# First layer's score maxima: one transpose of 24 columns per head pair and three small DMAs, in place of eight transposes of three columns

## The chip, the cores and the metric

The program runs on one core of a Trainium2 chip. The metric is the device time of one execution in microseconds. Matmuls and transposes run on TensorE (PE, its weight loads are shown as PEld), elementwise work on VectorE (DVE), ScalarE (ACT) and GpSimd (POOL); SyncE (SP) issues the DMAs.

## The reference

The input x is 8 sequences of 512 rows by 256 columns. Two layers follow each other: x + attention(layernorm(x)), x + ffn(layernorm(x)), and the same again with another attention and another ffn. What matters here is the first attention. It has 16 heads, queries of 96 values, and three sets of keys per head:

```python
a1 = _attn(q, k1, v1, causal=True)     # 512 latent keys
a2 = _attn(q, ks, vs, causal=False)    # 64 selected rows
a3 = _attn(q, kw, vw, causal=True)     # 512 window keys
out = g[:, 0] * a1 + g[:, 1] * a2 + g[:, 2] * a3
```

Each `_attn` is softmax(q k / sqrt(96)) v in float32, and a softmax over up to 512 keys must have its row's maximum (or something near it) taken off before the exponential. So there are 3 attentions x 2 heads x 4 blocks of 128 query rows = 24 columns of maxima for every pair of heads.

## The kernel before, in words

A hardware loop runs over the 8 sequences. Within a sequence the first attention goes by 8 pairs of heads, p = 0 to 7. Its scores are computed transposed: keys on the partitions, queries in the columns. A maximum therefore can't be taken off as a scalar per partition. It goes in as extra rows of the matmul: `QW[p % 2][0]` holds the queries' 96 values in partitions 0 to 95 (`D0` = 96), and in partitions 96, 97 and 98 the negated maxima of attentions A1, A3 and A2, each for 2 heads x 512 queries. The keys have a one in the row of their own attention, so that the 99-row product (L811) adds the negated maximum.

For pair p these are the steps:

- `max` (12 times, L774): scores of the pair in the other layout, of which DVE takes the maxima into `NMX[:, p % 2, 0:24]` (L1085, L1088, L1095). Column c = (attention * 2 + head) * 4 + query block.
- `mt` (`transpose_maxima`, L784): PE turns `NMX`. For each head there are four transposes of three columns (c, c + 8, c + 16), each of which writes 3 partitions x 128 columns of a bank of PSUM: 8 transposes in 2 banks.
- `mt_out` (`maxima_out`, L1419 for layer 1, through `copy` at L1340 for layer 0): ACT copies each bank (3 partitions x 512) straight into partitions 96 to 98 of `QW`.
- `unit` (12 times, L811 to L813): the transposed scores. Unit 0 of a pair waits first for the maxima to be in place, since it is the first to read them.
- ACT takes the exponential (L1445), POOL masks (L1573), and PE multiplies with the values (`pv`, L850).

Beside it, PE computes the next pair's queries and keys (`piece`, L731 to L745; their transposes `piece_tr`, L756). All engines walk the same list `STEPS[0]`, made once from numbers in `AFTER`: every engine has its own instructions of each step, in this order, and waits on semaphores. Within the list, what stands from `mt` up to the next `unit 0` is:

```
pair 0:       mt, tail_pe 3 (nothing), piece 2, mt_out, piece 3, piece_tr 0, unit 0
pairs 1 to 6: mt, piece 2, mt_out, unit 11 of the pair before, piece 3, pv 4, piece_tr 0, out, out, unit 0
pair 7:       mt, mt_out, unit 11 of the pair before, pv 4, out, out, unit 0
```

The banks of PSUM for scores and transposes are a ring of 5 (`Banks`): each use waits until the use 5 before it has been read. SP's queue in a sequence holds, in this order: the weights of pairs 1 and 2 (two DMAs of 256 KB each, L576 and L577), the store of the sequence before (512 KB, L573, in step `tail 3`, just ahead of `mt_out` of pair 0), and then the weights of pair p + 2 after piece 6 of each pair. `tail_pe` is the last layer of the sequence before, which is finished within the first attention of the next one.

Of the kernel before, what the change touches and what calls it, by code (L numbers as in the profile page):

```python
# [11 lines left out]
F32 = mybir.dt.float32  # L12
BF16 = mybir.dt.bfloat16
F32R = mybir.dt.float32r
# [243 lines left out]
def plan_banks():  # L258
    work, first, last = Banks(NWORK), Banks(NWORK), Banks(NWORK)

    def piece(banks, s):
        banks.use(s, 2 if s[0] == "piece_tr" or PIECES[s[2]][0] == "nv" else 4)

    def tail(banks, tag, j):
        for name in (["o0", "o1"], ["hT0", "hT1"], ["sign0", "sign1"], [])[j]:
            banks.use((tag, name))

    def prologue(banks, tag, j):
        for name in (["hT0", "hT1"], ["small0", "small1", "imp"], ["score_cols", "gate"], ["nqT", "ckvT"],
                     ["pos"], ["selT"])[j]:  # L270
            banks.use((tag, name))

    def attention(layer):
        for s in STEPS[layer]:
            if s[0] == "mt" and layer == 0:
                for h in range(2):
                    work.use((0,) + s + (h,))
            elif s[0] in ("unit", "max", "mt", "out_tr", "group"):
                work.use((layer,) + s, {"unit": 0, "mt": 2}.get(s[0], 1))
            elif s[0] in ("piece", "piece_tr"):  # L280
                piece(work, s)
            elif s[0] == "projection":
                for i in range(2):
                    work.use(("proj", i))
            elif s[0] == "pro_pe":
                prologue(work, "next", s[1])
            elif s[0] == "tail_pe":
                tail(work, "before", s[1])

    for j in range(6):  # L290
        prologue(first, "first", j)
    for m in range(NPIECE):
        piece(first, ("piece", 0, m))
        piece(first, ("piece_tr", 0, m))
    for j in range(4):
        tail(last, "last", j)
    work.of.update(first.of)
    work.of.update(last.of)
    attention(0)
    for i in range(2):  # L300
        work.use(("hT", 1, i))
    for s in FFN_STEPS:
        if s[0] == "pro_pe":
            prologue(work, "next", s[1])
        elif s[0] != "pro":
            work.use(s)
    for what, n in QKV_STEPS:
        if what == "half":
            work.use(("hT", 2, n))
        elif what == "v":  # L310
            work.use(("v", n))
        elif what == "qk":
            work.use(("qk1", n), 2)
        else:
            for k in range(4):
                work.use(("heads", n, k), 2 if k < 2 else 1)
    attention(1)
    return work

# [31 lines left out]
def build_program(nc, x, w_small, w_imp, w_q, w_nv, w_kw, w_sel, w_proj, g_q, g_kv,  # L351
# [4 lines left out]
    with ctx:  # L356
        def sb(name, shape, dt=F32):
            return ctx.enter_context(nc.sbuf_tensor(name, shape, dt))
# [67 lines left out]
        STATE = NRM[:, :].rearrange("p (i n a) -> p i n a", i=2, n=4)  # L426
        R2 = PR
        NMX = sb("NMX", [P, 2, 24])
        NPART = sb("NPART", [P, 2])
        RSUM = sb("RSUM", [P, 3, NT, 4])  # L430

# [11 lines left out]
        def sem(name):  # L443
            return ctx.enter_context(nc.semaphore(name))
# [15 lines left out]
        kr_ready = sem("kr_ready")  # L460
        tok_ready = sem("tok_ready")
        max_ready = sem("max_ready")
        exp_ready = sem("exp_ready")
        exp_masked = sem("exp_masked")
        evacuated = sem("evacuated")
# [21 lines left out]
        def full(e, use, bank):  # L487

            ring, sems, banks = bank
            k, _, f, _, _ = ring.of[use]  # L490
            e.wait_ge(sems[k], f)
            return banks[k]

        WORK = (work, work_full, WB)

        def maxima_uses(layer, p):
            return [(0, "mt", p, 0), (0, "mt", p, 1)] if layer == 0 else [(1, "mt", p)]

        def end_pass(e, n):

# [7 lines left out]
        def was_read(e, ring, sems, use):  # L508

            k, _, _, r, _ = ring.of[use]  # L510
            e.wait_ge(sems[k], r)
# [46 lines left out]
        @block.sync  # L558
        def _(sp):
            sp.dma_start(X0[:, :, :], x_rows[:, 0:NT, :]).then_inc(x_loaded, 16)  # L560
            for dst, src in early_loads:
                sp.dma_start(dst, src).then_inc(early_loaded, 16)

            def next_pass():

                sp.wait_ge(finished, 4)
                sp.sem_clear(cleared)
                sp.sem_inc(next_sequence, 1)

            def store(tag, row_tile):  # L570
                for i in range(2):
                    was_read(sp, work, work_read, (tag, f"sign{i}"))
                sp.dma_start(out_rows[:, bass.ds(row_tile, NT), :], X2[:, :, :]).then_inc(x_stored, 16)  # L573

            def load_weights(p):
                sp.dma_start(WKW[:, p % 2, :, :], w_kw[p % NPAIR]).then_inc(kw_loaded[p % 2], 16)  # L576
                sp.dma_start(WSEL[:, p % 2, :, :], w_sel[p % NPAIR]).then_inc(sel_loaded[p % 2], 16)  # L577

            load_weights(0)
            for dst, src in late_loads:  # L580
                sp.dma_start(dst, src).then_inc(late_loaded, 16)
            next_pass()
            with sp.Fori(0, B) as seq:
                for p in (1, 2):
                    load_weights(p)
                for s in STEPS[0]:
                    if s[0] == "piece" and s[2] == NPIECE - 1 and s[1] + 2 <= NPAIR:

                        full(sp, s, WORK)
                        load_weights(s[1] + 2)  # L590
                    elif s == ("tail", 3):

                        store("before", ((seq + (B - 1)) % B) * NT)

                for i in range(2):
                    was_read(sp, work, work_read, ("proj", i))
                sp.dma_start(X0[:, :, :], x_rows[:, bass.ds(((seq + 1) % B) * NT, NT), :]).then_inc(x_loaded, 16)
                next_pass()
            store("last", (B - 1) * NT)
            sp.wait_ge(x_stored, 16 * (B + 1))  # L600
            sp.wait_ge(x_loaded, 16 * (B + 1))
# [3 lines left out]
        def _(pe):  # L605
            mm = nc.tensor.matmul

            def take(use, bank):

                ring, full_sems, banks, read_sems = bank  # L610
                k, free_at, _, _, exp_at = ring.of[use]
                if exp_at > 0:
                    pe.wait_ge(exp_ready, exp_at)
                elif free_at > 0:
                    pe.wait_ge(read_sems[k], free_at)
                return banks[k], full_sems[k]
# [160 lines left out]
            def transpose_maxima(layer, p):  # L777
                if layer == 0:
                    pe.wait_ge(max_ready, p + 1)
                    for h in range(2):  # L780
                        ps, done = take((0, "mt", p, h), W)
                        for t in range(NT):
                            c = h * NT + t
                            last = nc.tensor.transpose(ps[0:3, t * P:(t + 1) * P], NMX[:, p % 2, c:24:8], ID[:, :])  # L784
                        last.then_inc(done, 1)
                else:
                    was_read(pe, work, work_read, (1, "max", p, len(MAX_UNITS[1]) - 1))
                    ps, done = take((1, "mt", p), W)
                    for t in range(NT):
                        last = nc.tensor.transpose(ps[0:2, t * P:(t + 1) * P], NMX[:, p % 2, t:8:NT], ID[:, :])  # L790
                    last.then_inc(done, 1)

            def unit(layer, p, i):

                if i == 0:

                    for use in maxima_uses(layer, p):
                        was_read(pe, work, work_read, use)
                ps, done = take((layer, "unit", p, i), W)
                for n_part, (a, h, j, col) in enumerate(UNITS[layer][i]):  # L800
                    q0, keys = j * P, (KEEP if layer == 0 and a == A2 else P)
# [197 lines left out]
        def _(dve):  # L999
# [71 lines left out]
            def maxima(layer, p, i):  # L1071
                u = MAX_UNITS[layer][i]
                ps = full(dve, (layer, "max", p, i), WORK)
                if i == 0 and layer * NPAIR + p >= 2:

                    full(dve, maxima_uses(*((layer, p - 2) if p >= 2 else (0, NPAIR - 2 + p)))[-1], WORK)
                for n, (lo, hi, att, h, qt) in enumerate(u["segs"]):
                    if att is None:
                        dst = NPART[:, h:h + 1]
# [256 lines left out]
        def _(act):  # L1336
# [72 lines left out]
                read_work(copy(dst[0], src), ("piece_tr", p, m))  # L1409

            def maxima_out(layer, p):
                for h in range(2):
                    if layer == 0:
                        ps = full(act, (0, "mt", p, h), WORK)
                        read_work(copy(QW[p % 2][0][D0:D0 + 3, h, :], ps[0:3, :]), (0, "mt", p, h))
                    else:
                        ps = full(act, (1, "mt", p), WORK)

                        read_work(a.activation(QZ[2 * D1:2 * D1 + 2, p, h, :], ps[0:2, :], ACT.Copy,  # L1419
                                               scale=ID[0:2, h:h + 1]), (1, "mt", p))  # L1420

            def outputs(layer, n, att):

# [291 lines left out]
```

## Time and profile before

| | us |
|---|---|
| median of 3 runs | 3653.43 |
| lowest, highest | 3652.27, 3654.14 |
| the profiled execution's own time | 3649.1 |
| its span | 3647.2 |

The span is from the first to the last instruction in the trace. An instruction is given by its line in the kernel, what it writes and reads, and its duration. A weight load (PEld) runs beside the matmul ahead of it, and a matmul's shown duration overlaps with the next one's: the distance from start to start tells what one costs. The granted clock of TensorE is given as a share of full speed.

### The profile page before, as it was taken

To read this page: it belongs to the slowest core of one execution; us is meant where nothing else is said; L and a number is where in the kernel's file an instruction comes from. 1 tells how busy PE (TensorE), PEld (TensorE's weight loads), DVE (VectorE), ACT (ScalarE), POOL (GpSimd) and SP (SyncE) were. 2 spreads that over 40 slices of the span, in tenths; PEclk is the share of its full clock that TensorE was granted. 3 is DMA by queue.
4 is the path that set the end of the run, shared out by engine and by line. 5 is a ranking of instruction groups with operands and counts; after the bars stand their busy time and mean duration, and the time that the engine had idled before them with its cause. 6 is when DMAs were issued, how large, how long until landed. Compare 5 with 4: busy or idle time off the path is not lost.

```text
span 3647.2 us, 58951 instructions
## 1 busy us (share of the span) xinstructions
PE 3255.5 (89%) x20560; PEld 2312.3 (63%) x20560; DVE 2121.1 (58%) x7104; ACT 1576.1 (43%) x3457; POOL 942.5 (26%) x1840
## 2 busy tenths in 40 slices
PE   4999789997899978998789988899788997899978
PEld 3776557765677646776467765677556765577655
DVE  3565655547556475665756656565665556556565
ACT  1444345533454334552444525445253542544434
POOL 0222222223222222222222222122221223222232
PEclk8999889998999989999899999999999998999989
DMA  2000000000000000000000000000001000000000
GB/s 90 24 14 12 1 13 24 18 7 1 19 18 19 7 1 25 18 13 7 1 25 19 13 7 1 30 18 7 6 1 30 19 7 6 13 18 19 13 0 7
DMA packets 31438, 53.75 MB, mean 15 GB/s; under 512 B 3472, under 2 KB 13456, under 8 KB 30864
## 3 DMA queue, kind: packets, MB, share of 16 engines
q1 hardware_dynamic: 31120, 49.64, 4.3%
q8 instruction: 183, 3.00, 0.4%
q14 instruction: 135, 1.11, 0.1%
HBM read 44.91 MB, written 4.72 MB: 14 GB/s over the span
## 4 chain that ended last, share of the span: by engine, by line
PE 77%; DVE 14%; issue 4%; POOL 3%; ACT 2%; SPq 0%; DMA 0%; ACTq 0%; DVEq 0%; POOLq 0%
PE outs L850 14%; PE work L774 7%; PE work L735 6%; PE work L811 6%; PE work L756 6%; PE work L812 5%; PE work L813 5%; PE work L857 4%; DVE work L1085 3%; PE work L731 3%; PE work L740 2%; PE work L635 2%; PE work L815 2%; PE work L745 2%; PE work L784 2%
## 5 line engine op out<-in xcount | busy, mean ns | idle before, releaser
L1445 ACT ACTIVATE PR<-work 128x512 f32<-128x512 f32 (+1 forms) x1088 | 640.0, 597 | 577.8 <-PE work L813 478.0
L1085 DVE CUSTOM_DVE_ANT_0 work<-work,KEEPB 128x384 f32<-128x384 f32 (+3 forms) x1536 | 665.4, 479 | 76.1 <-PE work L774 75.0
L1573 POOL TENSOR_SCALAR_AFFINE_SELECT PR<-PR 128x256 f32<-128x256 f32 (+1 forms) x960 | 348.1, 366 | 958.0 <-ACT PR L1445 954.0
L774 PE MATMUL work<-BIG 96*128 96x448 f32 (+9 forms) x1664 | 432.3, 354 | 71.2 <-issue 32.7
L1069 DVE TENSOR_TENSOR BIG<-work,BIG 96x512 fp32r<-96x512 f32 (+1 forms) x455 | 285.4, 629 | 351.1 <-ACT BIG L1340 351.1
L1563 POOL TENSOR_TENSOR TOK<-AB 128x256 f32<-128x256 f32 (+1 forms) x325 | 218.9, 674 | 867.7 <-DVE AB L1039 845.0
L850 PE MATMUL outs<-PR,ONES 128*32 128x512 f32 (+4 forms) x2304 | 404.6, 458 | 0.0
L811 PE MATMUL work<-BIG 99*128 99x512 f32 (+4 forms) x1152 | 404.5, 351 | 0.0
L774 PEld LDWEIGHTS work<-BIG 96*128 96x128 f32 (+1 forms) x1664 | 269.8, 196 | 205.0 <-issue 121.8
L1038 DVE TENSOR_TENSOR AB<-work,COS 128x256 f32<-128x256 f32 (+2 forms) x357 | 150.0, 420 | 429.3 <-PE work L735 368.1
L812 PE MATMUL work<-BIG 96*128 96x512 f32 (+4 forms) x1152 | 382.2, 332 | 0.0
L813 PE MATMUL work<-BIG 96*128 96x512 f32 (+4 forms) x1152 | 381.8, 331 | 0.0
L1340 ACT ACTIVATE BIG<-work 96x512 fp32r<-96x512 f32 (+2 forms) x583 | 315.7, 551 | 78.2 <-PE work L756 74.8
L850 PE MATMUL outs<-PR,VV 128*32 128x512 f32 (+3 forms) x2048 | 337.8, 440 | 0.0
L1340 ACT ACTIVATE TOK<-work 128x128 f32<-128x128 f32 (+1 forms) x455 | 122.6, 270 | 454.0 <-DVE AB L1039 242.6
L756 PEld LDWEIGHTS work<-ID,TOK 128*96 128x96 f32 (+1 forms) x1690 | 174.2, 126 | 162.3 <-issue 74.4
L735 PE MATMUL work<-WKW,HT 128*128 128x256 f32 x1040 | 277.0, 389 | 0.0
L756 PE MATMUL work<-ID,TOK 128*96 128x128 f32 (+1 forms) x1690 | 262.7, 275 | 14.4 <-ACT VV L1340 8.1
L811 PEld LDWEIGHTS work<-BIG 99*128 99x128 f32 (+1 forms) x1152 | 210.4, 183 | 40.4 <-issue 24.3
L813 PEld LDWEIGHTS work<-BIG 96*128 96x128 f32 (+1 forms) x1152 | 213.1, 185 | 23.7
L1088 DVE TENSOR_REDUCE NMX<-work 128x1 f32<-128x64 f32 (+1 forms) x640 | 172.3, 285 | 85.1 <-PE work L774 79.8
L812 PEld LDWEIGHTS work<-BIG 96*128 96x128 f32 (+1 forms) x1152 | 212.9, 185 | 5.0
(166 smaller groups left out, 5457.9 us busy)
## 6 DMA issues: line engine op xcount, KB each, us to landing
WKW<-w_kw_dram SPq DMA_DIRECT2D x65, 256.0 KB, 2.7
WSEL<-w_sel_dram SPq DMA_DIRECT2D x65, 256.0 KB, 3.0
X<-x_dram SPq DMA_DIRECT2D x9, 512.0 KB, 3.4
out_dram<-X SPq DMA_DIRECT2D x9, 512.0 KB, 2.9
WFC<-w_fc_dram SPq DMA_DIRECT2D x1, 1024.0 KB, 10.3
WFP<-w_ffp_dram SPq DMA_DIRECT2D x1, 1024.0 KB, 12.1
WQKV<-w_qkv_dram SPq DMA_DIRECT2D x1, 768.0 KB, 13.2
WQ<-w_q_dram SPq DMA_DIRECT2D x1, 576.0 KB, 7.2
```

Source lines behind the costliest of these rows:

```text
L735: last = mm(ps[:, 192:448], HT0[:, c, t * P:(t + 1) * P], WKW[:, p % 2, c, :], start=(c == 0), stop=(c == NC - 1))
L756: last = nc.tensor.transpose(ps[0:D0, h * rows:(h + 1) * rows], TOK[0:rows, (nth(p) * NPIECE + m) % 4, h, :], ID[0:rows, 0:rows])
L774: last = mm(ps[:, col:col + n], q, k, start=(i_mm == 0), stop=(i_mm == len(u["mm"]) - 1))
L811: mm(out, k[0][0:D0 + 3], q[0][0:D0 + 3], start=(col == 0), stop=False)
L812: mm(out, k[0][0:D0], q[1][0:D0], start=False, stop=False)
L813: last = mm(out, k[1][0:D0], q[0][0:D0], start=False, stop=stop)
L850: last = mm(bank[row:row + 32, j * P:T], v, PR[0:rows, slot, col:col + T - j * P], start=(j == 0), stop=(j == 2 or a == A2), skip_group_ch ...
L1069: read_work(v.tensor_tensor(dst[1], src, dst[0].bitcast(F32), ALU.subtract), use)
L1085: last = v.tensor_tensor_reduce(ps[:, lo:hi], ps[:, lo:hi], KEEPB[:, T - (hi - lo):T], -1.0, -NEG, ALU.add, ALU.min, dst)
L1340: return a.activation(dst, src, ACT.Copy)
L1445: a.activation(PR[0:rows, j % NP, :], ps[0:rows, :], ACT.Exp).then_inc(exp_ready, 1)
L1573: gp.affine_select(blocks, blocks, [[0, len(cols)], [1, P]], ALU.is_ge, 0.0, base=0, channel_multiplier=-1).then_inc(exp_masked, 1)
```

## The change

One transpose turns all 24 columns of `NMX` into 24 partitions x 128 columns of one bank. ACT copies these into a new tile `MROWS` (24 partitions, 2 buffers). SP waits for the copy and issues three DMAs from SBUF to SBUF: attention a has partitions 8a to 8a + 7 of `MROWS` (2 heads x 4 blocks, 128 values each, 512 bytes), which become one row of 1024 values, 4 KB, in partition 96 + a of `QW`. Unit 0 waits on their semaphore. The place of `mt`, `mt_out` and `unit` in `STEPS` is as before; SP gets a branch for `mt_out`. Layer 1 computes as before.

```diff
             def transpose_maxima(layer, p):
                 if layer == 0:
                     pe.wait_ge(max_ready, p + 1)
-                    for h in range(2):
-                        ps, done = take((0, "mt", p, h), W)
-                        for t in range(NT):
-                            c = h * NT + t
-                            last = nc.tensor.transpose(ps[0:3, t * P:(t + 1) * P], NMX[:, p % 2, c:24:8], ID[:, :])
-                        last.then_inc(done, 1)
+                    ps, done = take((0, "mt", p), W)
+                    nc.tensor.transpose(ps[0:24, 0:P], NMX[:, p % 2, :], ID[:, :]).then_inc(done, 1)
...
             def maxima_out(layer, p):
+                ps = full(act, (layer, "mt", p), WORK)
+                if layer == 0:
+                    if p >= 2:
+                        act.wait_ge(maxima_placed, MAXIMA_PLACED * (p - 1))
+                    read_work(copy(MROWS[:, p % 2, :], ps[0:24, 0:P]), (0, "mt", p))
+                    return
                 for h in range(2):
-                    if layer == 0:
-                        ps = full(act, (0, "mt", p, h), WORK)
-                        read_work(copy(QW[p % 2][0][D0:D0 + 3, h, :], ps[0:3, :]), (0, "mt", p, h))
...
+            def place_maxima(p):
+                was_read(sp, work, work_read, (0, "mt", p))
+                for a in range(3):
+                    sp.dma_start(QW[p % 2][0][D0 + a:D0 + a + 1, 0:2, :].bitcast(F32),
+                                 MROWS[8 * a:8 * a + 8, p % 2, :].bitcast(F32)).then_inc(maxima_placed, 16)
...
+                    elif s[0] == "mt_out":
+                        place_maxima(s[1])
...
             def unit(layer, p, i):
                 if i == 0:
-                    for use in maxima_uses(layer, p):
-                        was_read(pe, work, work_read, use)
+                    if layer == 0:
+                        pe.wait_ge(maxima_placed, MAXIMA_PLACED * (p + 1))
+                    else:
+                        was_read(pe, work, work_read, (1, "mt", p))
...
-            if s[0] == "mt" and layer == 0:
-                for h in range(2):
-                    work.use((0,) + s + (h,))
-            elif s[0] in ("unit", "max", "mt", "out_tr", "group"):
-                work.use((layer,) + s, {"unit": 0, "mt": 2}.get(s[0], 1))
+            if s[0] in ("unit", "max", "mt", "out_tr", "group"):
+                work.use((layer,) + s, {"unit": 0, "mt": 1 + layer}.get(s[0], 1))
```

`MAXIMA_PLACED` is 16 * 3, the semaphore's count for three DMAs.

## Rows read from the trace of the kernel before

**Rows 1.** The page: busy time (us, share, instructions) and the chain's shares

```profile
PE 3255.5 (89%) x20560; PEld 2312.3 (63%) x20560; DVE 2121.1 (58%) x7104; ACT 1576.1 (43%) x3457; POOL 942.5 (26%) x1840
...
PE 77%; DVE 14%; issue 4%; POOL 3%; ACT 2%; SPq 0%; DMA 0%; ACTq 0%; DVEq 0%; POOLq 0%
```

**Rows 2.** Stretches: from:to length, busy by engine (instructions), clock, DMA share, GB/s

```profile
551.93:579.54 27.61, 27.56 (x188) 20.12 (x187) 16.62 (x60) 15.33 (x37) 7.21 (x16) 1.00 0.12 39
579.54:610.83 31.29, 31.29 (x228) 22.33 (x227) 19.10 (x69) 15.55 (x38) 8.90 (x19) 1.00 0.06 18
```

**Rows 3.** Groups by line: busy us, mean ns of one

```profile
L1340 ACT ACTIVATE TOK<-work 128x128 f32<-128x128 f32 x390 | 108.5, 278 | 367.6 <-DVE AB L1039 240.7 <-issue 89.5 <-PE work L740 19.5
...
L784 PE MATMUL work<-ID,NMX 128*3 128x128 f32 x512 | 66.4, 273 | 0.0
```

**Rows 4.** Timeline around pair 1's maxima: start, us, instruction, [idle before <-releaser]

```profile
579.33 0.96 PEld L784 LDWEIGHTS work<-ID,NMX 128*3 128x3 f32 x8
579.54 1.04 PE L784 MATMUL work<-ID,NMX 128*3 128x128 f32 x8
...
580.50 0.52 PEld L740 LDWEIGHTS work<-WQ,NQT 32*128 32x128 f32 x4 [0.22 <-issue]
...
581.25 0.28 ACT L1340 ACTIVATE TOK<-work 128x128 f32<-128x128 f32 x1 [0.28 <-PE work L740]
...
581.72 1.06 ACT L1340 ACTIVATE BIG<-work 3x512 fp32r<-3x512 f32 x2
...
584.56 0.19 PEld L811 LDWEIGHTS work<-BIG 99*128 99x128 f32 x1
```

**Rows 5.** Timeline around pair 0's maxima

```profile
551.93 1.04 PE L784 MATMUL work<-ID,NMX 128*3 128x128 f32 x8
...
554.11 1.06 ACT L1340 ACTIVATE BIG<-work 3x512 fp32r<-3x512 f32 x2
...
555.24 0.19 PEld L811 LDWEIGHTS work<-BIG 99*128 99x128 f32 x1
```

**Rows 6.** Timeline around pair 7's maxima

```profile
766.05 1.04 PE L784 MATMUL work<-ID,NMX 128*3 128x128 f32 x8
...
766.25 0.59 ACT L1445 ACTIVATE PR<-work 64x512 f32<-64x512 f32 x1 [1.26 <-PE work L813]
...
766.87 1.06 ACT L1340 ACTIVATE BIG<-work 3x512 fp32r<-3x512 f32 x2
...
768.71 0.19 PEld L811 LDWEIGHTS work<-BIG 99*128 99x128 f32 x1 [0.41 <-issue]
```

**Rows 7.** Timeline of SP's queue: start of the issue, us that it took

```profile
520.67 0.33 SPq L576 DMA_DIRECT2D WKW<-w_kw_dram  x1
521.04 0.43 SPq L577 DMA_DIRECT2D WSEL<-w_sel_dram  x1
521.51 1.31 SPq L576 DMA_DIRECT2D WKW<-w_kw_dram  x1
522.87 0.43 SPq L577 DMA_DIRECT2D WSEL<-w_sel_dram  x1
```

**Rows 8.** DMAs from 551.9 to 554.9: busy tenths in 40 slices, queue, landing

```profile
DMA  0000000000002899999999999999998300000000
...
q1 hardware_dynamic: 528, 0.52, 49.3%
...
out_dram<-X SPq DMA_DIRECT2D x1, 512.0 KB, 2.8
```

**Rows 9.** All loads of L576 (256 KB each)

```profile
DMA to landing us min/median/max: 2.4/2.7/5.6
```

**Rows 10.** Stretches in the second layer with PE partly idle, columns as in rows 2

```profile
877.00:882.80 5.80, 2.40 (x20) 1.93 (x19) 2.45 (x4) 5.36 (x11) 4.05 (x5) 1.00 0.00 0
882.80:886.20 3.40, 3.39 (x16) 2.99 (x15) 0.69 (x1) 3.03 (x6) 0.00 (x0) 0.50 0.00 0
886.20:899.90 13.70, 8.35 (x42) 5.64 (x44) 12.56 (x48) 5.38 (x11) 1.18 (x4) 1.00 0.01 2
```

More of the change, by code:

```diff
@@ L428, in build_program @@
         NMX = sb("NMX", [P, 2, 24])
+        MROWS = sb("MROWS", [24, 2, P], F32R)
         NPART = sb("NPART", [P, 2])
@@ L462, in build_program @@
         max_ready = sem("max_ready")
+        maxima_placed = sem("maxima_placed")
         exp_ready = sem("exp_ready")
@@ L494, in build_program @@
         WORK = (work, work_full, WB)
-        def maxima_uses(layer, p):
-            return [(0, "mt", p, 0), (0, "mt", p, 1)] if layer == 0 else [(1, "mt", p)]
+        MAXIMA_PLACED = 16 * 3
         def end_pass(e, n):
@@ L1074, in maxima @@
                 if i == 0 and layer * NPAIR + p >= 2:
-                    full(dve, maxima_uses(*((layer, p - 2) if p >= 2 else (0, NPAIR - 2 + p)))[-1], WORK)
+                    full(dve, (layer, "mt", p - 2) if p >= 2 else (0, "mt", NPAIR - 2 + p), WORK)
                 for n, (lo, hi, att, h, qt) in enumerate(u["segs"]):
@@ L1411, in maxima_out @@
             def maxima_out(layer, p):
-                for h in range(2):
-                    if layer == 0:
-                        ps = full(act, (0, "mt", p, h), WORK)
-                        read_work(copy(QW[p % 2][0][D0:D0 + 3, h, :], ps[0:3, :]), (0, "mt", p, h))
[L1416 to L1420, printed above, removed]
+                ps = full(act, (layer, "mt", p), WORK)
[4 more added lines that the diff above has]
+                    return
+                for h in range(2):
+                    read_work(a.activation(QZ[2 * D1:2 * D1 + 2, p, h, :], ps[0:2, :], ACT.Copy,
+                                           scale=ID[0:2, h:h + 1]), (1, "mt", p))
             def outputs(layer, n, att):
```

## The prediction

> **What bounds the kernel now.** I read the page first: PE is busy 89% of the span and makes 77% of the chain that ended last, DVE 14% [rows 1]. An average can hide stages, so next came the view by stretches, cut at the maxima's transposes. There the first attention is seen to be PE's alone: of the 31.29 us from one pair's transposes to the next pair's, PE is busy for all 31.29, at the full granted clock (1.00, that is 2.4 GHz), while DVE has 19.10 and ACT 15.55; the first pair's stretch has 27.56 of 27.61 [rows 2]. So whatever PE no longer does in this stage comes off the end, and whatever PE waits for there is added. Then I read the timeline from `mt` to unit 0, once for each of the three orders in which the steps stand: pair 0, pairs 1 to 6, pair 7 [rows 4 to 6]. All 8 sequences repeat these distances within 0.03 us, so they stand for 8, 48 and 8 pairs.
>
> I call M the start of a pair's first transpose, and count from it. Everything that the change touches lies between M and the weight load of unit 0 (L811), because PE takes its instructions in order: what shifts that load shifts all after it. Before, the load comes at
>
> - pairs 1 to 6: 584.56 - 579.54 = 5.02 us [rows 4]. ACT's second copy is over at 581.72 + 1.06 = 582.78, at 3.24: PE does not wait for it, there are 1.78 us to spare.
> - pair 0: 555.24 - 551.93 = 3.31 us. The copies end at 555.17, and the load follows 0.07 us later: here PE waits for ACT, just so [rows 5].
> - pair 7: 768.71 - 766.05 = 2.66 us, the copies end at 1.88 [rows 6].
>
> **What is removed.** 7 of 8 transposes per pair. Eight starts lie in 1.04 us, of which the last one's own duration is 0.273 [rows 3, 4], so a start-to-start distance is (1.04 - 0.273) / 7 = 0.11 us, and seven are 0.77 us. Their matmuls' 273 ns each would give 1.91, but they overlap. The 0.2 us between the last transpose and the load of the next step [rows 4] stays: it follows one transpose as it follows eight. That the one left has 24 columns as weights instead of three changes its weight load only, which lies beside the matmul ahead of it; I cost it at nothing, and without that cover it would be some hundredths, 64 times. The gain, if nothing waits, is 64 x 0.77 = 49 us. Of the bank ring, `mt` takes one bank fewer, so the uses behind it wait for an older use than before: relaxed or equal, nothing. ACT has one copy of 128 columns in place of two of 512, which saves 0.78 us per pair on an engine with 15.55 of 31.29 busy: nothing by itself, but it ends sooner.
>
> **What is added: a chain between ACT's copy and unit 0.** Before, ACT wrote the rows itself. Now it is copy, semaphore, three issues on SP one after the other, landing of the last, semaphore, PE.
>
> *End of the copy.* ACT's queue ahead of it: in pair 1 its copy for piece 2 waits for L740 until 581.25 [rows 4]. With L740 0.77 earlier this copy can follow its predecessor (the row gives 0.28 idle before it), so the maxima's copy starts 0.28 earlier, at 1.90, and takes about the 0.278 of a 128x128 copy [rows 3]: end 2.17. Pair 0 has the same queue (554.11 - 551.93 = 2.18 at its start before) and the same end, 2.17. In pair 7 ACT is in an exponential until 766.84, so the copy starts at 0.82 as before and ends at 1.10 [rows 6].
>
> *The handoffs.* ACT's end to PE's load is 0.07 [rows 5]. I take that twice, for ACT to SP and for the landing to PE.
>
> *The issues.* Back to back, the second starts 0.37 after the first and the next one 0.47 later (520.67, 521.04, 521.51) [rows 7]: the third of three starts at 0.84. SP has nothing else then: the next weights are asked for after piece 6, behind unit 0, and in pair 0 the store ahead is issued at about M and its packets are over at 2.4 (551.9 + 32 slices of 0.075) [rows 8], while the first placing DMA, issued at 2.24, has its first packet 0.9 later. The rows are of DMAs over 128 partitions; for 8 source rows no row shows the issue. Its bounds are nothing at all and the 1.31 us that the third one took there; I take the 0.84, the commonest.
>
> *The landing.* No DMA within SBUF is in the trace. The nearest is the store, 512 KB out of SBUF in 528 packets: landed 2.84 us after its issue (2.8 in the row), of which each of the 16 engines had 49.3% of 3.0 = 1.48 us of packets [rows 8]. What is left, 1.36, is what no size takes away: the strip has nothing for 12 slices of 0.075, so 0.9 us until the first packet, and about 0.4 after the last. One packet of 1 KB is 1.48 / 33 = 0.045. A placing DMA has 8 packets of 512 bytes: on one engine 0.18 to 0.36, over several less. I take 0.20 and so a landing of 1.56. The floor is 1.4; the ceiling from the rows is the fastest load of 256 KB, 2.4 [rows 9], whose own packets it can do without. The Trainium skill (DMA: Bandwidth & Descriptors, Anatomy of one DMA) gives for DMAs issued by GpSimd a fixed cost of about 2.0 us for any small transfer. These are issued by SP, and the store's remainder of 1.36 speaks against it here; with 2.0 the sum would be that of the first rival below.
>
> The whole handoff is then H = 0.07 + 0.84 + 1.56 + 0.07 = 2.54 us from the copy's end, and unit 0's load comes at
>
> - pairs 1 to 6: 2.17 + 2.54 = 4.71, where PE would be ready at 5.02 - 0.77 = 4.25. It waits 0.46 of the 0.77 that it gained: 4.71 - 5.02 = -0.31.
> - pair 0: 4.71 against 3.31: +1.40. The transposes gain nothing here, since it was ACT's copy that ended last already, and the handoff is longer than the 0.78 us of copying that it replaces.
> - pair 7: 1.10 + 2.54 = 3.64 against 2.66: +0.98. There are no pieces between.
>
> The sum is 6 x (-0.31) + 1.40 + 0.98 = +0.52 us per sequence, 8 x 0.52 = +4 us. The profiled execution took 3649.1 around its span of 3647.2, so it would be 3653 with the change; it lies 4.3 below the median of the runs, and on that, 3653.4 + 4 = **3658 us** (rounded up). What is queued behind the waiting load on PE is everything else, and nobody else is late for it: DVE, ACT and POOL have 12 us or more to spare per pair [rows 2], and catch up while PE stands. Once PE waits, each 0.1 us of H moves 64 pairs: 6.4 us. That is the whole case. The balance is zero at H = 2.47, faster by the full 0.2% (7.3 us, what a measurement of this kernel can tell from no change) under 2.36, slower by it over 2.59.
>
> **The rivals.**
>
> 1. *Slower: the landing is longer than the store's remainder says.* It is decided at a landing of 1.6 us, where H passes 2.59. With 2.0, H is 2.98, unit 0's loads are at 5.15 and 4.08, and the shifts +0.13, +1.84, +1.42: 8 x 4.04 = +32 us, 3686. With 2.4 as in rows 9 it is +58 us, 3711; the same if SP holds the third issue as in rows 7. For it: the rows of loads [rows 9]. Against it: these wait for HBM's data, and move 64 times as much. The skill's fixed cost named above makes this rival's first figure.
> 2. *Faster: the small DMAs are cheap to issue or quick to land.* With H = 2.0 the maxima lie there at 4.17, before PE comes at 4.25: pairs 1 to 6 keep their 0.77, pair 0 has +0.86, pair 7 +0.44. 8 x (-4.62 + 1.30) = -27 us, 3627. With both at their floors (H = 1.5) it is -35 us, 3619. For it: an issue that handles 8 rows may have less to do than one of 128. Against: two of the four issues of rows 7 took the same 0.43 and none less than 0.33.
> 3. *Slower: the clock.* Pair 0's wait of 2.2 us comes a few us after the stage's begin. In the second layer PE had 2.40 us busy of 5.80, and then the granted clock was 0.50, that is 1.2 GHz, for 3.40 us; but in the 13.70 us behind it, with 8.35 busy, it was 1.00 [rows 10]. Pair 0 has no such gap ahead of its wait, so I think it unlikely. Its price is half of 3.4 us on each of 8 sequences: +14 on the forecast, 3672.
> 4. *The gain isn't there.* If another engine had to end first after all, pairs 1 to 6 gain nothing and the other two still lose: 8 x 2.38 = +19, 3672. A PE busy 31.29 of 31.29 [rows 2] speaks against it.
>
> **How the numbers follow.** The forecast, H from 2.3 to 2.75, so 3642 to 3671: 41%, of which 28 within 0.2%, 5 faster, 8 slower. Rival 1: 22%. Rival 2: 29%. Rival 3: 6%. Rival 4: 2%. Faster: 29 + 5 = 0.34; same 0.28; slower 8 + 22 + 6 + 2 = 0.38. The range: 3624 holds rival 2's figure and leaves its floor out, 3692 holds rival 1's first figure and leaves out the second. The forecast's own range is 3642 to 3671.
>
> **What would show it.** In pairs 1 to 6, L784 once per pair, L740's load 0.2 us after it, L811's load at M + 4.7 with PE idle 0.4 to 0.5 us before it and SP's DMA as releaser; at M + 4.7 in pair 0 and M + 3.6 in pair 7, with idle time of 2.2 and 1.8. Three issues of about 0.4 us on SP per pair, and a median landing near 1.6 us. The prediction is wrong if the landing is 1.9 or more, if the issues are far from 0.43 us, or if the granted clock is under 1.00 behind pair 0's wait.

## The result

The changed kernel takes 3734.14 us (median of 4 runs, 3733.89 to 3734.86), the one before 3653.43: ratio 1.022, 95% interval 1.020 to 1.024. It is 81 us slower; 3658 was forecast, with a range up to 3692. In the page, PE's share of the chain that ended last fell from 77% to 69% [rows 1], and a transfer stands in it:

```profile
PE 3285.7 (88%) x20112; PEld 2314.6 (62%) x20112; DVE 2114.1 (57%) x7104; ACT 1511.7 (41%) x3393; POOL 945.7 (25%) x1840
...
PE 69%; DVE 14%; issue 5%; DMA 3%; POOL 3%; ACT 3%; SPq 2%; ACTq 0%; DVEq 0%; POOLq 0%
```

The view of one tile, `MROWS`, shows what was added. The first line is SP's issues (duration min/median/max in ns), the second ACT's copy, the last two who waited and how long in all 64 pairs:

```profile
L576 SPq DMA_DIRECT2D BIG<-MROWS x192: 634/640/787, 109.9 to 3508.6; - x192
L1344 ACT ACTIVATE MROWS<-work x64: 250/258/258, 109.7 to 3507.0; 24x128 fp32r<-24x128 f32 x64
...
  PEld work L815: 85.7, 64
  PE work L815: 67.7, 64
```

The timeline around pair 1's maxima, which answers to [rows 4] (L784 is now L787, L811 is L815, L850 is L854):

```profile
594.39 0.27 PE L787 MATMUL work<-ID,NMX 128*24 128x128 f32 x1
...
596.02 0.26 ACT L1344 ACTIVATE MROWS<-work 24x128 fp32r<-24x128 f32 x1
596.30 2.01 SPq L576 DMA_DIRECT2D BIG<-MROWS  x3
599.48 0.19 PEld L815 LDWEIGHTS work<-BIG 99*128 99x128 f32 x1 [0.85 <-DMA BIG<-MROWS]
```

From M = 594.39, the copy ends at 1.89, SP issues from 1.91 to 3.92, and unit 0's load is at 5.09. It was at 5.02: PE made the transposes 0.77 us shorter and then waited 0.85. The same places of pair 0 and pair 7, against [rows 5, 6], whose loads stood at 3.31 and 2.66:

```profile
564.91 0.27 PE L787 MATMUL work<-ID,NMX 128*24 128x128 f32 x1
...
570.08 0.19 PEld L815 LDWEIGHTS work<-BIG 99*128 99x128 f32 x1 [2.69 <-DMA BIG<-MROWS]
```

```profile
781.22 0.27 PE L787 MATMUL work<-ID,NMX 128*24 128x128 f32 x1
...
781.92 0.25 ACT L1344 ACTIVATE MROWS<-work 24x128 fp32r<-24x128 f32 x1
...
782.19 2.01 SPq L576 DMA_DIRECT2D BIG<-MROWS  x3
...
785.36 0.19 PEld L815 LDWEIGHTS work<-BIG 99*128 99x128 f32 x1 [2.64 <-DMA BIG<-MROWS]
```

They are at 5.17 and 4.14: +1.86 and +1.48. Summed over a sequence, 6 x 0.08 + 1.86 + 1.48 = 3.8 us, and 31 us over eight. Most of the other 50 are in the next view, the stretches from pair 7's transpose on (columns as in [rows 2]):

```profile
781.22:787.10 5.88, 3.72 (x31) 2.01 (x33) 0.00 (x0) 3.05 (x7) 0.07 (x1) 1.00 0.01 2
787.10:797.40 10.30, 10.30 (x43) 6.72 (x38) 2.25 (x9) 2.36 (x4) 1.33 (x4) 0.50 0.01 2
797.40:821.30 23.90, 20.18 (x147) 13.83 (x145) 6.33 (x23) 6.95 (x12) 5.76 (x11) 1.00 0.00 0
```

From 1.7 us behind the wait the granted clock is 0.50 (1.2 GHz) for 10.3 us. PE is busy throughout and gets through 43 matmuls. Before, the first 10.30 us from this transpose held 78 at 1.00:

```profile
766.05:776.35 10.30, 10.30 (x78) 6.62 (x77) 2.20 (x9) 6.20 (x11) 1.40 (x4) 1.00 0.01 2
```

These are not the same matmuls. The same one, in the changed kernel (first line) and before (second):

```profile
787.69 1.07 PE L854 MATMUL outs<-PR,VS 64*32 64x512 f32 x2
```

```profile
770.77 0.60 PE L850 MATMUL outs<-PR,VS 64*32 64x512 f32 x2
```

An estimate from this: of 10.2 us at half clock with PE never idle, half is lost, 5 us per sequence.

From pair 7's transpose to the next pair 0's it takes 235.9 to 237.8 us (237.6 in the sequence shown) where it took 229.3 to 230.0: +7.4 us per sequence in the mean, of which 1.5 are the wait. Part of it comes later still. From 35 us behind pair 7's transpose to the next sequence's first, the mean granted clock is 0.87 (first line) where it was 0.89 (second, the kernel before):

```profile
816.22:1018.86 202.64, 162.44 (x791) 114.83 (x791) 123.83 (x382) 72.77 (x140) 50.24 (x84) 0.87 0.03 9
```

```profile
801.05:995.39 194.34, 157.11 (x783) 111.77 (x784) 119.46 (x365) 72.69 (x140) 48.64 (x82) 0.89 0.03 8
```

These stretches differ in length by 8.3 us since their starts are set by time and not by work; it is the sum over the whole way, here 8.3 us, that counts.

Two smaller parts lie inside the first attention. In two sequences the clock was low for 6.8 and 3.4 us behind pair 0's wait, 4.9 us together. In two, one of them the same, the last of pair 5's three DMAs landed 3.0 and 3.1 us after its issue in place of 1.76, and PE waited 2.1 and 2.2 us there in place of 0.85; the clock stayed at 1.00 behind these.

### The profile page after: what moved, and what is told of

Same layout as the page of the kernel before. It is cut to its first block, busy times and chain, and to the rows that moved or that the text cites. A ratio compares the mean times of both kernels' runs of the same rounds, so it can differ in the third digit from the quotient of the medians.

```text
span 3732.4 us, 58231 instructions
## 1 busy us (share of the span) xinstructions
PE 3285.7 (88%) x20112; PEld 2314.6 (62%) x20112; DVE 2114.1 (57%) x7104; ACT 1511.7 (41%) x3393; POOL 945.7 (25%) x1840
## 4 chain that ended last, share of the span: by engine, by line
PE 69%; DVE 14%; issue 5%; DMA 3%; POOL 3%; ACT 3%; SPq 2%; ACTq 0%; DVEq 0%; POOLq 0%
PE outs L854 13%; PE work L780 7%; PE work L815 6%; PE work L816 5%; PE work L741 5%; PE work L817 5%; PE work L762 5%; PE work L861 4%; DMA BIG<-MROWS 3%; DVE work L1089 3%; SPq L576 2%; PE work L641 2%; PE work L737 2%; PE work L751 2%; PE work L819 2%
## 5 line engine op out<-in xcount | busy, mean ns | idle before, releaser
L815 PE MATMUL work<-BIG 99*128 99x512 f32 (+4 forms) x1152 | 412.7, 358 | 67.7 <-DMA BIG<-MROWS 67.7
L854 PE MATMUL outs<-PR,ONES 128*32 128x512 f32 (+4 forms) x2304 | 416.1, 469 | 0.0
L780 PEld LDWEIGHTS work<-BIG 96*128 96x128 f32 (+1 forms) x1664 | 274.3, 200 | 202.8 <-issue 122.2
L816 PE MATMUL work<-BIG 96*128 96x512 f32 (+4 forms) x1152 | 388.4, 337 | 0.0
L817 PE MATMUL work<-BIG 96*128 96x512 f32 (+4 forms) x1152 | 387.5, 336 | 0.0
L854 PE MATMUL outs<-PR,VV 128*32 128x512 f32 (+3 forms) x2048 | 343.0, 445 | 0.0
L815 PEld LDWEIGHTS work<-BIG 99*128 99x128 f32 (+1 forms) x1152 | 215.7, 187 | 123.7 <-DMA BIG<-MROWS 85.7
L1344 ACT ACTIVATE BIG<-work 96x512 fp32r<-96x512 f32 (+1 forms) x455 | 248.1, 545 | 76.0 <-PE work L762 74.2
L817 PEld LDWEIGHTS work<-BIG 96*128 96x128 f32 (+1 forms) x1152 | 218.1, 189 | 24.1
L816 PEld LDWEIGHTS work<-BIG 96*128 96x128 f32 (+1 forms) x1152 | 218.0, 189 | 5.0
```

Of the source, the lines that this page charges most:

```text
L780: last = mm(ps[:, col:col + n], q, k, start=(i_mm == 0), stop=(i_mm == len(u["mm"]) - 1))
L815: mm(out, k[0][0:D0 + 3], q[0][0:D0 + 3], start=(col == 0), stop=False)
L816: mm(out, k[0][0:D0], q[1][0:D0], start=False, stop=False)
L817: last = mm(out, k[1][0:D0], q[0][0:D0], start=False, stop=stop)
L854: last = mm(bank[row:row + 32, j * P:T], v, PR[0:rows, slot, col:col + T - j * P], start=(j == 0), stop=(j == 2 or a == A2), skip_group_ch ...
L1344: return a.activation(dst, src, ACT.Copy)
```

## The experiments

The kernel before was run again beside each group of experiments, with medians of 3651.8 to 3652.1 us; "before" below is that of the same group, and the rows of a sequence are from the profiled execution.

In the first two, one pair of each sequence keeps the old way, chosen by a tuple, `(7,)` in the first and `(0,)` in the second:

```diff
+OLD = (7,)
...
-                    elif s[0] == "mt_out":
+                    elif s[0] == "mt_out" and s[1] not in OLD:
                         place_maxima(s[1])
```

**Pair 7 the old way.**

> The changed kernel, but pair 7 of each sequence keeps the eight transposes and ACT's direct copies. In the trace of the changed kernel unit 0's weight load stands at M + 5.10 in pairs 1 to 6 (5.02 before), M + 5.17 in pair 0 (3.31 before) and M + 4.14 in pair 7 (2.66 before), which adds up to 8 x (0.5 + 1.86 + 1.48) = 31 us; measured are 81. Theory A: the other 50 us come from the granted clock, which is 0.50 for 10.2 us just behind pair 7's wait of 2.6 us (and 1.00 in the same place before); then from pair 7's transpose to the next pair 0's it takes 229.3 us again instead of 237.6, which takes 8 x 8.3 = 66 us off: 3668. Rival B: the 50 us are a price of the DMAs or of the changed order that does not hang on pair 7's wait; then only 8 x 1.48 = 12 us go: 3722.

Measured: 3709.16 us, 25 less than the changed kernel, between the two. Theory A's own place is right: from pair 7's transpose to the next pair 0's it takes 231.1 us in place of 237.6, more than the wait's 1.48, though not the 229.3 of before: farther behind there are still 48 to 55 us at half clock per sequence, where the kernel before had 41 to 48. And the low clock had moved. In seven of the eight sequences 6.8 us of it now lie behind pair 0's wait, where the kernel before had none and the changed one had some in two of eight:

```profile
559.90:566.60 6.70, 4.27 (x23) 3.34 (x22) 2.20 (x5) 2.23 (x9) 1.78 (x3) 1.00 0.23 80
566.60:573.40 6.80, 6.80 (x22) 4.45 (x21) 1.98 (x4) 2.60 (x8) 1.36 (x3) 0.50 0.00 1
```

So pair 0 to pair 1 took 32.6 us against 29.5, which ate half of what pair 7 gave.

**Pair 0 the old way.**

> The changed kernel, but pair 0 of each sequence keeps the eight transposes and the direct copies. Theory A: only pair 0's 1.86 us go, 8 times: 3719, and the low clock behind pair 7 stays. Rival C: it is pair 0's wait of 2.7 us, right behind a stretch at half clock, that unsettles the clock for the whole sequence; then some 50 + 15 us go: 3669.

Measured: 3710.5 us, 24 less: 15 for the wait and 9 more. Pair 0 to pair 1 is 27.6 us again, and behind pair 7 the low clock is 6.8 us in six of eight sequences, where it was 10.2 in six of eight. Neither theory's number; pair 0's wait too has a part in how much low clock there is.

**No wait at all.** The DMAs go aside:

```diff
-                    sp.dma_start(QW[p % 2][0][D0 + a:D0 + a + 1, 0:2, :].bitcast(F32),
+                    sp.dma_start(QW[p % 2][1][D0 + a:D0 + a + 1, 0:2, :].bitcast(F32),
...
-                    if layer == 0:
-                        pe.wait_ge(maxima_placed, MAXIMA_PLACED * (p + 1))
...
+                        for use in maxima_uses(layer, p):
+                            was_read(pe, work, work_read, use)
+                if i == 6 and layer == 0:
+                    pe.wait_ge(maxima_placed, placed(p))
```

`maxima_uses` is the copy that ACT made of the transpose. PE's wait for the DMAs now stands six units later, where the trace shows nobody waiting for them; `placed(p)` is the same count as before.

> The changed kernel with its one transpose, one copy and three DMAs per pair, but the DMAs write into unused partitions 96 to 98 of the queries' low part, the row of maxima is zero, and unit 0 waits for ACT's copy alone: the maxima are not taken off, so part of the computation is left out. Theory A: without the wait only the transposes' gain is left, 0.77 us in each of 64 pairs, 49 us: 3604, with the clock in the first attention at 1.00 throughout. Rival B: if issuing and moving the DMAs, or the relaxed ring of banks, costs something itself, it stays above 3640.

Measured: 3610.68 us, 41 less than before. Pair to pair it is 30.50 us where it was 31.27, so each pair has its 0.77, and PE is never idle:

```profile
574.31:604.82 30.51, 30.51 (x221) 21.67 (x219) 19.11 (x69) 14.40 (x37) 8.90 (x19) 1.00 0.06 19
```

Pairs 1 to 6 pay nothing for their issues and transfers when nobody waits for them, so rival B is out. Of theory A's 49 us 8 are missing: unit 0's load came 0.85 us earlier in pair 0 but only 0.4 of it reached pair 1, and behind the first attention two of the seven ways to the next sequence took 231.1 us where the others took about 228, with 55 us at half clock in place of 41 to 48. Whether the DMAs have a part in that isn't shown.

**One DMA of 24 rows.**

```diff
-                for a in range(3):
-                    sp.dma_start(QW[p % 2][0][D0 + a:D0 + a + 1, 0:2, :].bitcast(F32),
-                                 MROWS[8 * a:8 * a + 8, p % 2, :].bitcast(F32)).then_inc(maxima_placed, 16)
+                sp.dma_start(QW[p % 2][0][D0:D0 + 3, 0:2, :].bitcast(F32),
+                             MROWS[:, p % 2, :].bitcast(F32)).then_inc(maxima_placed, 16)
```

> The changed kernel, but one DMA takes all 24 partitions of 128 values to the 3 rows of 1024 in place of three DMAs. In the changed kernel the third is issued 1.38 us after the first and lands 1.76 us after its issue. Theory A: one issue, landing in about 1.8 us, gives a handoff of 1.9 us from the copy's end: pairs 1 to 6 wait for nothing and keep 0.77 us, pair 0 shifts by +0.5, pair 7 by +0.2 with a wait of under 1 us that leaves the clock at 1.00: 8 x (-4.6 + 0.7) = -32 us, 3622. Rival D: the issue and the landing grow with the number of rows, so that one DMA of 24 rows costs what three of 8 do, landing 2.5 us or more: pairs 1 to 6 at M + 4.5, pair 0 +1.2, pair 7 +0.9: about 3645. Rival B: a fixed price of the DMAs, 3670 or more.

Measured: 3625.60 us, ratio 0.994, interval 0.992 to 0.995: 26 us faster than before, 109 faster than the change with three DMAs. Issue and landing grow only a little with the rows. Pair 1, then pair 0 (issue, load):

```profile
581.18 0.74 SPq L585 DMA_DIRECT2D BIG<-MROWS  x1
583.50 0.19 PEld L833 LDWEIGHTS work<-BIG 99*128 99x128 f32 x1
```

```profile
552.72 0.79 SPq L585 DMA_DIRECT2D BIG<-MROWS  x1
554.96 0.19 PEld L833 LDWEIGHTS work<-BIG 99*128 99x128 f32 x1 [1.69 <-DMA BIG<-MROWS]
```

Pair 1's load comes 4.23 us after M = 579.27 and waits for nothing. In pair 0, where PE is there first, the load follows the issue by 2.24 us; 1.69 us of waiting are left and in pair 7 1.62, and behind both the clock stays at 1.00. Theory A's course, then, with a landing that is longer than its 1.8: pair 0 is at +0.86 and pair 7 at +0.45, so 8 x (-6 x 0.79 + 1.31) = -27 us. One of the seven executions took 3646.1 us at a mean granted clock of 0.933, where the others had 3622.5 to 3627.1 and 0.945 to 0.949. It has no profile; it may be that the low clock came back in it.

**Both pairs the old way** (`OLD = (0, 7)`, three DMAs in pairs 1 to 6).

> The changed kernel's one transpose and three DMAs in pairs 1 to 6 only; pairs 0 and 7 keep the eight transposes and the direct copies. Taking one of the two pairs back recovered 25 and 24 us of 81, and in the trace with pair 7 taken back the low clock had moved: 6.8 us at 0.50 behind pair 0's wait, which were not there with both changed. Theory A: each of the two waits can pull the clock down, the loss is both together; with both gone the first attention runs at 1.00 and what is left are 48 times the 0.08 us of pairs 1 to 6: 3656 against 3652. Rival B: 20 us or more of the loss come from the waits of 0.85 us in pairs 1 to 6 or from the DMAs themselves: 3675 or more.

Measured: 3662.0 us, ratio 1.0026, interval 1.0016 to 1.0036: 10 us, not 4. Theory A, with an addition. In two of eight sequences pair 5 took 3.1 us more. 1.4 of them are a longer wait, 2.3 us in place of 0.85, and the rest a low clock of 3.4 us right behind it (second line of the windows):

```profile
1598.90:1602.90 4.00, 1.98 (x23) 0.84 (x21) 1.44 (x3) 1.96 (x5) 0.73 (x1) 1.00 0.03 7
1602.90:1606.40 3.50, 3.50 (x9) 2.90 (x10) 0.00 (x0) 0.60 (x1) 0.00 (x0) 0.51 0.00 0
```

```profile
1598.27 2.01 SPq L586 DMA_DIRECT2D BIG<-MROWS  x3
1602.87 0.20 PEld L834 LDWEIGHTS work<-BIG 99*128 99x128 f32 x1 [2.27 <-DMA BIG<-MROWS]
```

The issues took their 2.01 us as ever; it is the third DMA that landed 3.2 us after its issue in place of 1.76. The DMAs from 1598 to 1604 have one packet beside those of the maxima, 16 KB of the instruction queue:

```profile
q8 instruction: 1, 0.02, 1.0%
```

Such a packet falls beside pair 5's DMAs in all eight sequences of this run and of the changed kernel, and takes about 1 us. In six of eight the landing is 1.76 all the same. That it holds up the landing in the other two is thus likely, not shown.

**Pair 7 alone the new way** (`OLD = (0, ..., 6)`).

> The kernel before in pairs 0 to 6; only pair 7 has the one transpose, the copy into the new tile and the three DMAs. Theory A: PE's wait of 2.6 us there shifts unit 0 by 1.48 us and is followed by a stretch of 7 to 10 us at half clock in which PE is never idle, so that from pair 7's transpose to the next pair 0's it takes 236 to 238 us in place of 229.6: 8 x 7 to 8 = 56 to 64 us, about 3712. Rival E: the low clock needs the waits of the pairs ahead as well; then 8 x 1.48 = 12 us, 3664.

Measured: 3693.92 us, +42, of which the wait is 12. In seven of eight sequences there are 6.8 us at half clock just behind the wait, and the way to the next pair 0 takes 234.4 to 236.9 us; in the one where the clock stayed it takes 231.45, which is the 229.6 of before plus 1.5 for the wait and 0.4. So rival E is out: one such wait per sequence is enough, though it costs less than theory A's 60.

**Pair 0 alone the new way.**

> The counterpart of the run with pair 7 alone: the kernel before in pairs 1 to 7, and only pair 0 has the one transpose, the copy and the three DMAs. Theory A: PE's wait of 2.7 us shifts unit 0 by 1.86 us, 8 times 15 us, and as with pair 7 the low clock adds more than the wait itself: 6.8 us at 0.50 behind it (3.1 us) and some 8 us more of it later in the sequence: 3690 to 3700. Rival I: a wait in pair 0 alone leaves the clock as it was, since the rows of the second layer show 1.00 behind waits as long: 3667.

Measured: 3684.53 us, +33, of which the wait is 15. Behind the wait the clock was low in only one of eight sequences (32.7 us against 29.5), so that part of theory A is wrong. The rest came late: the way behind pair 7, which had not changed, took 231.2 us in place of 229.7 and had 51 to 55 us at half clock in place of 41 to 48. Why a shift of 1.86 us at pair 0 brings more low clock 250 us later is not settled.

**Four shapes of DMA**, the wait moved out of the way as above (a single execution, of which only the issues are read):

> Nobody waits for the placing DMAs here (as in the run without the wait, the maxima are not taken off: part of the computation is left out), and SP issues four of them per pair, each of another shape: 8 source rows to one row of 1024 values, 8 rows to 8 rows, 16 rows to 16 rows, 24 rows to 24 rows, all of 512 bytes per source row. It is to tell what makes an issue of these take 0.64 us where those of 128 rows took 0.43. Theory F: it is the number of engines that a DMA uses, below 16 of them the issue costs more; then 16 rows take about 0.43 and 8 rows about 0.64 to either destination, and 24 rows (8 engines) about 0.7. Rival G: it is the source in SBUF or the unequal shapes: then 16 rows take 0.64 too, or 8 to 8 takes 0.43.

The four lines below are the issues of 8 rows to one row, 8 to 8, 16 to 16 and 24 to 24:

```profile
L586 SPq DMA_DIRECT2D BIG<-MROWS x64: 642/660/788, 111.8 to 3391.9; - x64
...
L587 SPq DMA_DIRECT2D BIG<-MROWS x64: 645/646/667, 112.7 to 3392.6; - x64
...
L588 SPq DMA_DIRECT2D BIG<-MROWS x64: 543/544/557, 113.4 to 3393.3; - x64
...
L589 SPq DMA_DIRECT2D BIG<-MROWS x64: 746/749/1457, 114.0 to 3393.9; - x64
```

8 rows cost 0.65 us to either destination, so the unequal shapes are not it. 16 rows cost less than 8 or 24, as theory F has it, but 0.54 and not 0.43, so something else than the number of engines must cost a tenth. And theory F's 8 engines for 24 rows do not fit the trace: it has 12 packets of 4 bytes behind the data there, where it has 8 for 8 rows and 16 for 16, which would be 12 engines, and their issue costs more than that of 8 (0.75 against 0.65). The one DMA of 24 rows into 3 rows has 3 such packets and took 0.73. The number of engines alone thus does not order the issues; what does, these runs do not tell.

**One DMA and earlier places for pairs 0 and 7.**

```diff
-        at += [(t, ("mt", p)), (t + 0.4, ("mt_out", p))]
+        out = 0.4
+        if layer == 0 and p in (0, NPAIR - 1):
+            t, out = t - {0: 0.93, NPAIR - 1: 0.5}[p], {0: 0.15, NPAIR - 1: 0.03}[p]
+        at += [(t, ("mt", p)), (t + out, ("mt_out", p))]
```

> One transpose and one DMA of 24 rows per pair, and the steps of two pairs moved in the list: pair 0's mt stands in front of the last layer's matmuls (tail_pe 2, 4.6 us of PE) and its mt_out ahead of the store in SP's queue; pair 7's mt and mt_out stand in front of unit 10 of pair 6 in place of behind it. With one DMA and the old places it was 3625.6, with waits of 1.7 and 1.6 us left in pairs 0 and 7. Theory A: the handoff of 2.2 us is then hidden in all 64 pairs and all keep their 0.77 us: 49 us less than before, 3603 to 3606. Rival H: DVE isn't done with the maxima at the earlier places, PE waits for it there, and half of the rest is lost again: 3615 or more.

Measured: 3595.33 us, ratio 0.985, interval 0.983 to 0.986: the fastest, 57 us under the kernel before. Pairs take 30.49 us, all PE's:

```profile
571.30:601.79 30.49, 30.49 (x220) 21.72 (x219) 19.10 (x69) 14.40 (x37) 8.93 (x19) 1.00 0.06 19
```

Pair 0 waits no more, and pair 7 0.6 us:

```profile
752.23 0.28 PE L807 MATMUL work<-ID,NMX 128*24 128x128 f32 x1
...
755.01 0.19 PEld L836 LDWEIGHTS work<-BIG 99*128 99x128 f32 x1 [0.59 <-DMA BIG<-MROWS]
```

Rival H is out. 57 us are 8 more than the 49 that all 64 pairs can keep; where these come from isn't shown.

**The earlier places with eight transposes.**

> Splits the fastest version (one transpose and one DMA, steps of pairs 0 and 7 moved, 3595) in two: the eight transposes and the direct copies in every pair, as before, but with pair 0's and pair 7's mt and mt_out at the moved places. Theory A: the moved places only hide the new handoff; by themselves they give back ACT's 0.07 us in pair 0 and cost or gain little else: 3648 to 3656, so that nearly all of the 57 us belong to the one transpose. Rival J: pair 0's transposes in front of the last layer's matmuls fill a gap in which PE waited anyway, so part of the 57 us (those beyond 49) comes from the places alone: 3640 to 3645.

Measured: 3650.96 us, ratio 1.000, interval 0.999 to 1.001: the places alone are worth nothing, so rival J is out. With one transpose they are worth 30 us (3625.6 to 3595.3). 22 of these are the waits that they hide, 1.69 us in pair 0 and 1.03 in pair 7, 8 times; the other 8 are those that stayed open above.

## Why the prediction was wrong, point by point

- *PE bounds the first attention, and what it waits for is added*: right. Where the clock stayed at 1.00, what PE no longer did and what it waited for came out of the pair's time to 0.1 us, except in pair 0 without the wait, where 0.4 of 0.85 did.
- *Seven transposes are 0.77 us*: right, measured without the wait (31.27 to 30.50).
- *The end of the copy* at 2.17 and 1.10: it was 1.89 and 0.94. ACT came to this copy sooner than I took it to. That helped by 0.28 and 0.16.
- *The issues*, the first step that failed: 0.84 us to the third one's start, from 0.37 and 0.47 in [rows 7]. Measured are three issues in 2.01 us of 0.64 each, so the third starts at 1.38. I had written that no row shows an issue of 8 rows and took the commonest anyway.
- *The landing*, 1.56: measured 1.76. In the strip below, 40 slices of 0.08 us from the first issue, the packets of the three DMAs stand at 1.28, 1.92 and 2.64. The first packet comes 1.28 us behind the start of its issue, where the store had 0.9 [rows 8]; what I put behind it was rather too much, the packets being over in 0.1 us and the load 0.4 us behind the last of them. Most of the later first packet is the longer issue once more: it comes 0.64 us after the end of a 0.64 us issue, and the store's came 0.54 after the end of one of 0.40 (second view). The Trainium skill (DMA: Bandwidth & Descriptors, Anatomy of one DMA) gives a fixed cost of about 2.0 us for GpSimd's DMAs; the trace shows 1.76 for a whole one of SP's.

```profile
DMA  0000000000000000200000001100000002000000
```

```profile
551.90 0.40 SPq L573 DMA_DIRECT2D out_dram<-X  x1
```

- The handoff was thus 3.21 us against 2.54. Less the earlier copy, this makes 31 us where 4 were forecast, about what the first rival had for a landing of 2.0 (+32), and still within the range.
- *The clock*, the step that put it outside: the third rival had the mechanism, 6% of chance and 14 us, and only pair 0. I argued that pair 0 has no other gap ahead of its wait, and never put the question for pair 7, though I had its wait at 1.8 us (2.1 as the view counts it, with the 0.41 us of [rows 6] that PE sat idle there anyway). It fell to 0.50 behind pair 7's 2.6 us, for 10.2 us in a stretch in which PE is the bound, and more of it came behind. 81 - 31 = 50 us; some 3 of these are the late landings in pair 5. That the two waits, each alone, cost 42 and 33 us, most of it more than the wait, shows that the clock is the larger half. That in the profiled execution of the one DMA, with waits of 1.8 us or less, it stayed at 1.00 shows it from the other side, though which of two waits gets it depends on more than their length.

What stays open: why a wait lowers the clock in one sequence and not in the next, and which of the places behind the first attention get the low clock. The same instructions had from 38 to 58 us at half clock per sequence, from kernel to kernel and from sequence to sequence.

## What to carry to other kernels

A short step that is replaced by copy, issue and landing is worth its gain only where the user is further behind than the whole handoff; measure that distance in every order in which the steps stand, the first and the last round too, since two pairs of eight made nearly the whole loss here. Where PE is never idle at full clock, a single wait of 2.6 us can cost much more than the shift that it makes (42 us for 12). Count the issues of small DMAs, not their bytes: one of 24 rows gave back 109 us against three of 8.

## What the runs showed of the hardware that I had not expected

- SP's issue of a DMA within SBUF took 0.65 us for 8 source rows, 0.54 for 16, 0.75 for 24, and 0.33 or 0.43 for the loads of 128 rows from HBM. 8 rows to one row of 4 KB cost the same as 8 to 8.
- The first packet of these transfers within SBUF came 0.64 us (median) after the end of the issue, of whatever shape, so a longer issue is a later landing.
- A 4 KB transfer within SBUF landed 1.76 us after the start of its issue, one of 12 KB in a single DMA 2.2 until PE's load. In pair 5 of two sequences in eight it was 3.0 to 3.2, with a 16 KB packet of instructions beside it.
- PE's clock in the profiled executions. Behind pair 7's waits of 2.6 to 2.7 us it was 0.50 in all eight sequences of the changed kernel and in seven of eight with pair 7 alone. Behind pair 0's of 2.7 us it was so in two of eight of the changed kernel, in seven of eight with pair 7 taken back, in one of eight with pair 0 alone. Behind pair 5's of 2.3 us it was so in both cases with pairs 0 and 7 taken back, with pair 0 alone taken back behind a wait of 2.35 but not behind one of 2.6, and in the changed kernel behind neither of 2.1 and 2.2. Behind waits of 1.8 us or less in the first attention it never was. The length of the wait alone does not tell.
